# Expert outputs added into two sums by token in main memory, in place of four stored rows a token

## The chip, the cores and the metric

The kernel runs on one core of a Trainium2 chip. The metric is the device time of one execution in microseconds (us). Three timed runs of the kernel before gave 1543.5 us in the median (1541.84 to 1544.97).

## The reference, cut to what matters

The program is a network of four layers on 32 sequences of 128 tokens with 128 features (4096 tokens). Each layer is a gated cross-attention and a gated feed-forward part. The change is in the last feed-forward part, a mixture of 16 experts of which every token uses four:

```python
dist2 = jnp.sum((x[:, :, None, :] - keys) ** 2, axis=-1)
logits = -dist2 + jnp.einsum('bld,ed->ble', x, rw) + rb
topv, topi = jax.lax.top_k(logits, 4)
w = jax.nn.softmax(topv, axis=-1)
hidden = gelu(jnp.einsum('bld,efd->blef', x, w1) + b1)      # 16 experts, 512 wide
exp_out = jnp.einsum('blef,edf->bled', hidden, w2) + b2
fused = jnp.sum(w[..., None] * take_along_axis(exp_out, topi), axis=2)
x = x + tanh(g_ffn[3]) * fused
```

## The kernel before, in words

The stages are called A0, F0, A1, F1, A2, F2, A3, F3 (attention and feed-forward of layers 0 to 3). Each works on eight chunks c of four sequences (512 tokens), with the activations `x` held on chip. There is no scheduler: every engine has its own program, written out by hand, and they meet at semaphores. All loads and stores of plain blocks stand in SP's queue, in the order of its program. POOL issues the indirect DMAs.

**Routing** (`routing`, steps u = 6 to 14, on PE, ACT, DVE and POOL) runs beside A3, one chunk late. It picks four experts for each token, gives each of the four copies a place in a region of main memory that belongs to its expert (`dispatched_rows`), and POOL sends the rows there (`send`, L806, 16 indirect DMAs of 128 rows a chunk). A row is 128 features and one integer, the row of `expert_outputs` where its result belongs. The last chunk is done in two halves; the second one, called `routing(NC, ..., 1)`, runs inside F3. Steps 12 and 13 compute the places and release the send (`F3_rows_ready`), steps 12 and 14 the softmax weights, kept in `wt3`. The regions must be filled with an invalid row number first. SP does that with `prefill`: six regions of 2128.5 KB beside the stages before A2, and ten more right before the context loads of A2 (L532).

**F3** treats 144 tiles of 128 rows, each of one expert, in 12 groups of 12 slots. SP loads a tile (`load_tile`, L578). PE transposes it (`tile_T`, L1494), multiplies by the first weights (`up`, L1500) and by the second (`down`, L1508). DVE copies each tile's weights into place three tiles ahead (`weights`, L2752 to L2757) and adds the second bias when it takes the result (`output`, L2766). POOL scatters the result to `expert_outputs` (`scatter`, L843), one row for each token and expert, so no two scatters touch the same row. A slot is loaded again when its group of four scatters has landed.

**The end.** When all scatters have landed, SP loads the four rows of every token (L600, 8 loads of 1024 KB). For four chunks DVE does 16 multiply-adds each (L2806). For the four others, named in `MIXED3`, ACT builds 16 diagonal matrices of weights (`diagonals`, L1962), PE sums through them (L1548) and DVE adds the bank (L2800). SP stores each chunk of `x` (L605).

Of the kernel before, what the change touches and what calls it, by code (L numbers as in the profile page):

```python
# [5 lines left out]
F32 = mybir.dt.float32  # L6
# [8 lines left out]
B = 32  # L15
# [29 lines left out]
ROW3 = P + 1  # L45
# [23 lines left out]
MIXED3 = (1, 3, 5, 7)  # L69
# [72 lines left out]
def flamingo(nc, a, out):  # L142
    ctx = ExitStack()
    with ctx:
# [41 lines left out]
        mhalf = sb("mhalf", [P, CB])  # L186
        rstd = sb("rstd", [P, CB])
# [174 lines left out]
        wt3 = ar([P, B * TOP3])  # L362
# [18 lines left out]
        combined = arena[:, 0:NC * TOP3 * W].rearrange("p (c j k d) -> p c j k d", c=NC, k=TOP3, j=CB)  # L381
# [22 lines left out]

        def tile_bank(s):

            return bank[7 if s % 2 else 4]
# [13 lines left out]
        def diagonal(i, q):  # L421

            if i % 2 == 0:
                return flat_wqk3[:, q, :]
            return (flat_wv3 if q < SC // 2 else flat_wo3)[:, q % (SC // 2), :]

        sent = nc.dram_tensor("dispatched_rows", (UNUSED + P, ROW3), F32, kind="Internal").ap()
        sent_out = nc.dram_tensor("expert_outputs", (TOP3 * TOKENS, P), F32, kind="Internal").ap()
# [76 lines left out]
        def _(sp):  # L505
# [87 lines left out]
            for half in range(SLOTS3 // GROUP3):  # L593
                sp.wait_ge(sem(f"F3_scattered{half}"), GROUPS3 * GROUP3 * 16)
# [4 lines left out]
            for c in range(NC):  # L599
                sp.dma_start(combined[:, c, :, :, :].rearrange("t j k d -> t j (k d)"),  # L600
                             sent_out[c * W * TOP3:(c + 1) * W * TOP3, :].rearrange("(j t k) d -> t j (k d)", t=P, k=TOP3))\
                    .then_inc(sem(f"F3_outputs_loaded{c}"), 16)
# [7 lines left out]
        def _(pl):  # L610
# [13 lines left out]
            pl.memset(padf3[:, 0:P], 0.0)  # L624
            pl.memset(padu3[:, P:P + 1], int(NOWHERE)).then_inc(sem("F3_pad_row"), 1)
# [160 lines left out]
            pl.iota(goes3[:, :].rearrange("p (j k) -> p j k", j=CB), pattern=[[P * TOP3, CB], [1, TOP3]], base=0, channel_multiplier=TOP3,  # L786
# [44 lines left out]
            pl.wait_ge(sem("F3_prefilled"), 16 * (E3 + 1))  # L831
# [7 lines left out]
            def scatter(g, slots):  # L839
                for s in slots:  # L840
                    pl.wait_ge(sem("F3_output"), g * SLOTS3 + (s + 3))
                    pl.sem_inc(s_held, 1)
                    pl.indirect_dma_start(sent_out, bass.IndirectOffsetOnAxis(xtu3[:, s, P:P + 1], 0), yt3[:, s, :], None,  # L843
                                          bounds_check=TOP3 * TOKENS - 1, oob_is_err=False).then_inc(sem(f"F3_scattered{s // GROUP3}"), 16)
# [8 lines left out]
            send(range(SC // 2), 0)  # L853
            scatter(0, range(GROUP3))
# [10 lines left out]
        def _(pe):  # L865
# [675 lines left out]
            for i, c in enumerate(MIXED3):  # L1541
                pe.wait_ge(sem(f"F3_outputs_loaded{c}"), 16)
                pe.wait_ge(sem("F3_diagonals"), i + 1)
                if i >= 2:
                    pe.wait_ge(s_xdone, NC * STAGE["F3"] + 2 + MIXED3[i - 2])
                for j in range(CB):
                    for k in range(TOP3):
                        last = nc.tensor.matmul(bank[4 + i % 2][:, j * P:j * P + P], diagonal(i, j * TOP3 + k), combined[:, c, j, k, :],  # L1548
                                                start=(k == 0), stop=(k == TOP3 - 1))
                last.then_inc(sem("F3_mixed"), 1)  # L1550
# [3 lines left out]
        def _(act):  # L1554
# [399 lines left out]
            def diagonals(i):  # L1954

                if i >= 2:
                    act.wait_ge(sem("F3_mixed"), i - 1)
                if MIXED3[i] == NC - 1:
                    act.wait_ge(sem("F3_last_weights"), 1)
                for q in range(SC):  # L1960
                    at = MIXED3[i] * SC + q
                    last = nc.scalar.activation(diagonal(i, q), ident[:, :], ACT.Copy, scale=wt3[:, at:at + 1])  # L1962
                last.then_inc(sem("F3_diagonals"), 1)

# [28 lines left out]
            routing(NC, 10, 1)  # L1993
            for i in range(len(MIXED3)):
                diagonals(i)
# [3 lines left out]
        def _(dve):  # L1999
# [68 lines left out]
            def routing(c, u, half=None):  # L2068
                js = ALL if half is None else HALVES[half]
                n, of, qs = len(js), slice(js[0], js[-1] + 1), qs_of(js)  # L2070
                at, (_, tags, places) = route_bank(c, half), rows_of(half)
# [28 lines left out]
                if u == 10:  # L2100
# [5 lines left out]
                    if half is None:  # L2106
                        v.tensor_scalar(goes3[:, :], goes3[:, :], float(W * TOP3), None, ALU.add)
# [9 lines left out]
                if u in (12, 13):  # L2117
# [8 lines left out]
                    v.tensor_copy(places[:, qs], to3[:, qs]).then_inc(sem("F3_rows_ready"), 1)  # L2126
                if u in (12, 14):
# [4 lines left out]
                    kept = wt3[:, bass.ds(c * SC, SC)] if half is None else wt3[:, chunk * SC + qs.start:chunk * SC + qs.stop]  # L2132
                    last = v.tensor_tensor(kept.rearrange("p (j k) -> p j k", j=n), ex3[:, of, :],
                                           es3[:, of].unsqueeze(2).to_broadcast([P, n, TOP3]), ALU.mult)
                    if half == 1:
                        last.then_inc(sem("F3_last_weights"), 1)
                    else:
                        step(last)
# [127 lines left out]
            def heads3():  # L2266
# [47 lines left out]
                def last_body(c):  # L2314
                    for w in range(PAIRS):
# [3 lines left out]
                        if w in (3, 4, 5, 6, 7):  # L2319
                            routing(c - 1, {3: 7, 4: 8, 5: 9, 6: 10, 7: 13}[w])  # L2320
# [8 lines left out]
                def drain(c):  # L2329
                    routing(c - 2, 14)  # L2330
# [416 lines left out]
            def weights(n, s):  # L2747
# [7 lines left out]
                v.tensor_copy(b2c3[:, s % 4, :], b2b3[:, bass.ds(e * P, P)])  # L2755
# [4 lines left out]
            def output(n, s, g):  # L2760
# [3 lines left out]
                if g is not None:  # L2764
                    dve.wait_ge(sem(f"F3_scattered{s // GROUP3}"), g * (16 * GROUP3))
                v.tensor_tensor(yt3[:, s, :], bank[2 + s % 2][:, 0:P], b2c3[:, s % 4, :], ALU.add).then_inc(sem("F3_output"), 1)  # L2766
# [3 lines left out]
            for s in range(SLOTS3):  # L2770
# [5 lines left out]
                if s == 2:  # L2776
                    routing(NC, 13, 1)
# [7 lines left out]
            with dve.Fori(1, GROUPS3 - 1) as g:  # L2785
                for s in range(SLOTS3):
                    weights(g * SLOTS3 + (s + 3), s + 3)
# [7 lines left out]
            routing(NC, 14, 1)  # L2795

            for c in range(NC):
                if c in MIXED3:
                    dve.wait_ge(sem("F3_mixed"), MIXED3.index(c) + 1)
                    v.tensor_tensor(xc(c), xc(c), b4(4 + MIXED3.index(c) % 2), ALU.add).then_inc(s_xdone, 1)  # L2800
                    continue
                dve.wait_ge(sem(f"F3_outputs_loaded{c}"), 16)
                for k in range(TOP3):
                    for j in range(CB):
                        q = c * SC + j * TOP3 + k
                        last = v.scalar_tensor_tensor(xc(c)[:, j, :], combined[:, c, j, k, :], wt3[:, q:q + 1], xc(c)[:, j, :], ALU.mult, ALU.add)  # L2806
                    if k < TOP3 - 1:
# [31 lines left out]
```

## Time and profile before

| | before |
|---|---|
| median of 3 runs | 1543.5 us |
| the profiled execution | 1540.11 us |
| its span, first to last instruction | 1538.3 us |
| PE busy | 1364.3 us (89%) |
| DVE busy | 1107.5 us (72%) |
| POOL busy | 539.1 us (35%) |
| 144 scatters on POOL | 145.9 us busy, 120.6 us idle before them |
| DMA traffic | 98.30 MB |

The engines are PE (matrix products), DVE (vector), ACT (scalar functions), POOL and SP. Idle time of an engine that nobody waits for costs nothing, so the rows below are read by stage: which wait ends last there.

### The profile page before, as it was taken

How to read it: one execution, taken by the hardware profiler on the slowest of the kernel's cores; microseconds unless marked ns; L12 is line 12 of the kernel's file. 1: busy time of each engine (PE TensorE's matmuls, PEld its weight loads, DVE VectorE, ACT ScalarE, POOL GpSimd, SP SyncE). 2: the span in 40 equal slices, each digit the busy share in tenths (PEclk: the TensorE clock that was granted, in tenths of full speed). 3: DMA queues.
4: the chain of work that ended last, by engine and by line, in shares of the span. 5: the costliest groups of instructions: out<-in, count | busy, mean ns of one | idle time of the engine just before them, and what ended most of it. 6: DMA issues, size and time to landing. Idle time of an engine off the chain costs nothing.

```text
span 1538.3 us, 34321 instructions
## 1 busy us (share of the span) xinstructions
PE 1364.3 (89%) x9959; PEld 1021.1 (66%) x9982; DVE 1107.5 (72%) x3553; ACT 1001.9 (65%) x2922; POOL 539.1 (35%) x640
## 2 busy tenths in 40 slices
PE   4788887899989988999899999999997779999994
PEld 3566665677744456444566666666666679999994
DVE  4778888688777757886467777777778656666665
ACT  2688887554556556224777888888876446666665
POOL 3354359222211321001001522423423665555550
PEclk9999999999999999999999999999999899999998
DMA  8100039900199961000000100100032322222227
GB/s 200 26 8 7 8 56 161 140 0 1 49 169 161 165 102 35 1 0 0 8 9 1 36 24 13 36 23 14 29 142 112 89 72 66 64 67 67 64 59 274
DMA packets 143416, 98.30 MB, mean 64 GB/s; under 512 B 20597, under 2 KB 132514, under 8 KB 142154
## 3 DMA queue, kind: packets, MB, share of 16 engines
q1 hardware_dynamic: 134602, 80.09, 27.8%
q0 software_dynamic: 8704, 16.87, 3.3%
q8 instruction: 54, 0.88, 0.2%
q14 instruction: 56, 0.46, 0.1%
HBM read 43.03 MB, written 54.93 MB: 64 GB/s over the span
## 4 chain that ended last, share of the span: by engine, by line
PE 65%; ACT 12%; DVE 9%; issue 8%; POOL 3%; DMA 2%; SPq 1%; DVEq 0%; ACTq 0%; POOLq 0%
PE bank L1056 7%; PE bank L1500 7%; PE bank L1508 7%; PE bank L1072 4%; PE bank L1350 4%; ACT arena L1555 4%; PE bank L997 3%; ACT att L1692 3%; PE bank L1111 3%; PE bank L1060 3%; PE bank L1092 3%; ACT att L1557 2%; PE bank L1082 2%; PE bank L1426 2%; PE bank L979 2%
## 5 line engine op out<-in xcount | busy, mean ns | idle before, releaser
L1555 ACT ACTIVATE arena<-bank 128x512 f32<-128x512 f32 (+7 forms) x380 | 245.6, 675 | 150.2 <-PE bank L1413 54.1
L1972 ACT ACTIVATE att<-bank,arena 128x128 f32<-128x128 f32 x576 | 164.2, 368 | 89.9 <-PE bank L1500 89.9
L843 POOL DMA_INDIRECT expert_outputs<-arena x144 | 145.9, 1013 | 120.6 <-DVE arena L2766 102.8
L1692 ACT ACTIVATE att<-bank,arena 128x128 f32<-128x128 f32 x512 | 180.2, 394 | 11.6 <-DVE arena L2271 11.3
L806 POOL DMA_INDIRECT dispatched_rows<-arena x112 | 114.9, 1025 | 162.7 <-DVE arena L2126 114.0
L1500 PE MATMUL bank<-xnT,arena 128*128 128x128 f32 x1152 | 155.9, 279 | 3.7 <-DVE arena L2757 3.7
L639 POOL TENSOR_TENSOR ve<-mv,eps 128x4 f32<-128x4 f32 x64 | 12.8, 200 | 416.7 <-DVE mv L2042 407.3
L1508 PE MATMUL bank<-arena,att 128*128 128x128 f32 x1152 | 154.4, 278 | 0.3 <-ACT att L1972 0.3
L1500 PEld LDWEIGHTS bank<-xnT,arena 128*128 128x128 f32 x1152 | 143.4, 196 | 4.4 <-issue 3.1
L1508 PEld LDWEIGHTS bank<-arena,att 128*128 128x128 f32 x1152 | 142.4, 195 | 0.5 <-ACT att L1972 0.5
L1692 ACT ACTIVATION_READ_ACCUMULATOR att<-bank,arena 128x1 f32 x512 | 120.2, 235 | 0.0
L2752 DVE COPY arena<-arena 128x512 f32 x144 | 62.3, 433 | 78.7 <-issue 77.7
L1555 ACT ACTIVATE xnT<-bank 128x128 f32<-128x128 f32 (+1 forms) x180 | 63.6, 354 | 77.6 <-PE bank L881 41.5
L2271 DVE TENSOR_REDUCE arena<-bank 128x4 f32<-128x512 f32 x128 | 82.4, 685 | 43.9 <-PE bank L1072 43.9
L1677 ACT ACTIVATE arena<-bank 128x512 f32<-128x512 f32 x128 | 75.9, 613 | 55.5 <-PE bank L1056 55.5
L997 PE MATMUL bank<-ident,att 128*128 128x128 f32 x512 | 70.9, 283 | 32.5 <-ACT att L1557 32.0
L2156 DVE TENSOR_REDUCE nmx<-bank 128x8 f32<-128x1024 f32 x64 | 78.0, 1219 | 26.4 <-PE bank L968 25.9
L2277 DVE TENSOR_TENSOR att<-att,arena 128x512 f32<-128x512 f32 x128 | 89.2, 697 | 4.4
L997 PEld LDWEIGHTS bank<-ident,att 128*128 128x128 f32 x512 | 57.2, 144 | 49.4 <-ACT att L1557 48.7
L1350 PE MATMUL bank<-arena 128*128 128x512 f32 x192 | 87.6, 592 | 1.3 <-ACT arena L1555 0.9
L1072 PE MATMUL bank<-arena 64*128 64x128 f32 x1024 | 74.4, 284 | 12.9 <-ACT att L1692 6.5
L1072 PEld LDWEIGHTS bank<-arena 64*128 64x128 f32 x1024 | 62.3, 187 | 33.5 <-issue 24.8
(412 smaller groups left out, 3204.5 us busy)
## 6 DMA issues: line engine op xcount, KB each, us to landing
dispatched_rows<-padf SPq DMA_DIRECT2D x16, 2128.5 KB, 35.4
arena<-dispatched_rows SPq DMA_DIRECT2D x144, 64.5 KB
cxT<-in_ctx SPq DMA_DIRECT2D x32, 256.0 KB, 2.8
arena<-in_L_ffn_w SPq DMA_DIRECT2D x8, 1024.0 KB
arena<-expert_outputs SPq DMA_DIRECT2D x8, 1024.0 KB, 13.2
expert_outputs<-arena POOLq DMA_INDIRECT x144
out_x<-x SPq DMA_DIRECT2D x8, 256.0 KB, 4.2
dispatched_rows<-arena POOLq DMA_INDIRECT x112
```

The source lines that it names most:

```text
L806: pl.indirect_dma_start(sent, bass.IndirectOffsetOnAxis(places[:, q:q + 1], 0), held[:, q, :], None)\
L843: pl.indirect_dma_start(sent_out, bass.IndirectOffsetOnAxis(xtu3[:, s, P:P + 1], 0), yt3[:, s, :], None, bounds_check=TOP3 * TOKENS - 1, o ...
L997: last = nc.tensor.transpose(bank[2 + k][:, i * P:i * P + P], ex[:, v % 2 * 2 + k, i, :], ident[:, :])
L1056: last = nc.tensor.matmul(A[:, :], wqk3[:, t, pair * P:pair * P + P], cxT[:, p, :] if t else xnT[:, :], start=True, stop=True)
L1072: last = nc.tensor.matmul(bank[side][:, i * P:i * P + P], q, k, start=True, stop=True)
L1350: last = nc.tensor.matmul(bank[1 + j][:, :], xsT1[:, p * CB + j, t:t + P], wconv1[:, t, :], start=False, stop=(t == 2))
L1500: last = nc.tensor.matmul(bank[s % 2][:, k * P:k * P + P], w1c3[:, s % 4, k * P:k * P + P], xnT[:, (s % 4) * P:(s % 4) * P + P], start=Tru ...
L1508: last = nc.tensor.matmul(bank[2 + s % 2][:, 0:P], h3[:, s % 2, k * P:k * P + P], w2c3[:, s % 4, k * P:k * P + P], start=(k == 0), stop=(k ...
L1555: copy = lambda o, i: nc.scalar.activation(o, i, ACT.Copy)
L1692: last = nc.scalar.activation(ex3_of(w, side)[:, i, :], bank[side][:, i * P:i * P + P], ACT.Exp, bias=nm3[:, w % 2, h:h + 1], accum_out=su ...
L1972: last = nc.scalar.activation(h3[:, s % 2, k * P:k * P + P], bank[s % 2][:, k * P:k * P + P], ACT.Gelu, bias=b1c3[:, s % 4, k:k + 1])
L2277: v.tensor_tensor(ex3_of(w, side), ex3_of(w, side), rs3[:, w % 2, side:2 * HQ:2].unsqueeze(2).to_broadcast([P, HQ, P]), ALU.mult) .then_in ...
```

## The change

Results are weighted before they leave the chip, and the scatters add. A dispatched row has one more word, the weight, so routing computes the weights before it releases a send. DVE multiplies the result and the bias by the weight of each row. There are two sums of 4096 rows in main memory, filled with zeros by SP behind the ten regions. A scatter adds its rows into one of them, in turn by slot. Two additions into one sum may not overlap, so each scatter waits until the last but one has landed. At the end 16 loads of 256 KB bring in the two sums, and DVE adds them to `x`. The diagonals, PE's sums and the multiply-adds of the end are gone. The exponential of the last half chunk goes from ACT, after the tiles, to POOL, before its first scatter.

```diff
-ROW3 = P + 1
+ROW3 = P + 2
+SUMS3 = 2
+        def wait_scattered(eng, g, s):
+            last = s // SUMS3 + 1
+            if not isinstance(g, int):
+                eng.wait_ge(sem(f"F3_scattered{s % SUMS3}"), g * (16 * SLOTS3 // SUMS3) + 16 * last)
+            elif g * SLOTS3 // SUMS3 + last > 0:
+                eng.wait_ge(sem(f"F3_scattered{s % SUMS3}"), 16 * (g * SLOTS3 // SUMS3 + last))
...
                     prefill(range(PREFILLED_F0, E3))
+                    for view in sums_view:
+                        sp.dma_start(view, padf3[:, 0:P].unsqueeze(1).to_broadcast([P, B, P])).then_inc(sem("F3_prefilled"), 16)
...
                 for s in range(SLOTS3):
-                    if s % GROUP3 == 0 and not (isinstance(g, int) and g == 0):
-                        sp.wait_ge(sem(f"F3_scattered{s // GROUP3}"), g * (16 * GROUP3))
+                    if not (isinstance(g, int) and g == 0):
+                        wait_scattered(sp, g, s - SLOTS3)
                     load_tile(g * SLOTS3 + s, s)
...
             for c in range(NC):
-                sp.dma_start(combined[:, c, :, :, :].rearrange("t j k d -> t j (k d)"), ...
+                for k in range(SUMS3):
+                    sp.dma_start(summed3[:, c, k, :, :], sums_view[k][:, c * CB:(c + 1) * CB, :]).then_inc(sem(f"F3_outputs_loaded{c}"), 16)
...
                     pl.wait_ge(sem("F3_output"), g * SLOTS3 + (s + 3))
                     pl.sem_inc(s_held, 1)
-                    pl.indirect_dma_start(sent_out, bass.IndirectOffsetOnAxis(xtu3[:, s, P:P + 1], 0), yt3[:, s, :], None,
+                    wait_scattered(pl, g, s - SUMS3)
+                    pl.sem_inc(s_held, 1)
+                    pl.indirect_dma_start(sums_out[s % SUMS3], bass.IndirectOffsetOnAxis(xtu3[:, s, P:P + 1], 0), yt3[:, s, :], None,
+                                          bounds_check=TOKENS - 1, oob_is_err=False, compute_op=ALU.add)
...
             send(range(SC // 2), 0)
+            pl.wait_ge(sem("F3_less_max"), NC + 1)
+            pl.tensor_tensor(ex3[:, CB // 2:CB, :], base_e[:, :].rearrange("p (j k) -> p j k", k=TOP3), top3[:, CB // 2:CB, 0:TOP3], ALU.pow)
             scatter(0, range(GROUP3))
...
-                v.tensor_copy(b2c3[:, s % 4, :], b2b3[:, bass.ds(e * P, P)])
+                dve.wait_ge(sem(f"F3_tiles_loaded{slot // GROUP3}"), turn * (16 * GROUP3) + 16 * GROUP3)
+                v.tensor_scalar(b2c3[:, s % 4, :], b2b3[:, bass.ds(e * P, P)], xt3[:, slot, P + 1:P + 2], None, ALU.mult)
...
-                v.tensor_tensor(yt3[:, s, :], bank[2 + s % 2][:, 0:P], b2c3[:, s % 4, :], ALU.add)
+                v.scalar_tensor_tensor(yt3[:, s, :], bank[2 + s % 2][:, 0:P], xt3[:, s, P + 1:P + 2], b2c3[:, s % 4, :], ALU.mult, ALU.add)
...
             for c in range(NC):
+                for k in range(SUMS3):
+                    last = v.tensor_tensor(xc(c), xc(c), summed3[:, c, k, :, :], ALU.add)
```

On POOL, where F3 begins, before: the sends of the last chunk's first half, then four scatters (`expert_outputs`), four sends of the second half, and so on.

```order
L806 DMA dispatched_rows<-arena,last_places 67712x129 [waits F3_rows_copied,F3_rows_ready]
L806 DMA dispatched_rows<-arena,last_places 67712x129 x7
L843 DMA expert_outputs<-arena 16384x128 [waits F3_output] x4
L806 DMA dispatched_rows<-arena,last_places 67712x129 [waits F3_rows_copied,F3_rows_ready]
L806 DMA dispatched_rows<-arena,last_places 67712x129 x3
L843 DMA expert_outputs<-arena 16384x128 [waits F3_output] x4
```

The same place now:

```order
L811 DMA dispatched_rows<-arena,last_places 67712x130 [waits F3_rows_copied,F3_rows_ready]
L811 DMA dispatched_rows<-arena,last_places 67712x130 x7
L863 TENSOR_TENSOR arena<-base_e,arena 128x8 [waits F3_less_max]
L850 DMA expert_sums<-arena 4096x128 [waits F3_output] x2
L850 DMA expert_sums<-arena 4096x128 [waits F3_output,F3_scattered0]
L850 DMA expert_sums<-arena 4096x128 [waits F3_output,F3_scattered1]
L811 DMA dispatched_rows<-arena,last_places 67712x130 [waits F3_rows_copied,F3_rows_ready]
L811 DMA dispatched_rows<-arena,last_places 67712x130 x3
```

The power (L863) stands between the sends and the first scatter, and from the third scatter on each waits for an earlier one's landing.

On SP, before A2's loop of context loads (`cxT`), before:

```order
L523 DMA cxT<-in_ctx 128x4x128 [waits A12_v] x2
L532 DMA dispatched_rows<-padf 128x33x129 x10
L548 UNCONDITIONAL_BRANCH
L548 ISA
L523 ISA [waits A12_v]
L523 DMA cxT<-in_ctx 128x4x128
```

and now:

```order
L526 DMA cxT<-in_ctx 128x4x128 [waits A12_v] x2
L535 DMA dispatched_rows<-padf 128x33x130 x10
L552 DMA expert_sums<-padf 4096x1x128 x2
L553 UNCONDITIONAL_BRANCH
L553 ISA
L526 ISA [waits A12_v]
L526 DMA cxT<-in_ctx 128x4x128
```

Two fills of 2 MB stand ahead of the context load of A2's third chunk.

On DVE, the places of the last but one chunk (to `arena`, L2126), followed by the copy of an attention bank that PE waits for (L2285), before:

```order
L2124 TENSOR_TENSOR arena<-arena 128x256 [waits vector_steps]
L2125 TENSOR_REDUCE arena<-arena 128x16 [waits vector_steps]
L2126 CAST arena<-arena 128x16 [waits vector_steps]
L2285 COPY arena<-bank 128x512 [waits A3_pv]
L2276 RECIPROCAL arena<-arena 128x4 [waits A3_exp]
```

and now (the copy is L2266):

```order
L2111 TENSOR_TENSOR arena<-arena 128x256 [waits vector_steps]
L2112 TENSOR_REDUCE arena<-arena 128x16 [waits vector_steps]
L2113 CAST arena<-arena 128x16 [waits vector_steps]
L2115 TENSOR_REDUCE arena<-arena 128x4 [waits F3_exp,vector_steps]
L2116 RECIPROCAL arena<-arena 128x4 [waits vector_steps]
L2117 TENSOR_SCALAR arena<-arena,gates 128x4 [waits vector_steps]
L2118 TENSOR_TENSOR arena<-arena 128x16 [waits vector_steps]
L2266 COPY arena<-bank 128x512 [waits A3_pv]
L2257 RECIPROCAL arena<-arena 128x4 [waits A3_exp]
```

The four weight instructions, which stood behind the statistics of the next half, now stand between the places and PE's copy, and the send is released behind them.

## Rows read from the trace of the kernel before

**Rows 1.** Stretches: us, PE, PEld, DVE, ACT, POOL busy, clock, DMA share, GB/s

```profile
428.00:540.00 112.00, 101.93 (x456) 53.98 (x465) 82.04 (x316) 67.13 (x131) 25.74 (x44) 0.98 1.28 164
1300.00:1480.00 180.00, 180.00 (x1617) 179.98 (x1616) 120.00 (x476) 124.12 (x476) 96.50 (x95) 1.00 0.24 67
1510.00:1526.00 16.00, 10.21 (x71) 10.02 (x72) 11.54 (x39) 7.95 (x28) 0.00 (x0) 0.77 1.04 388
1528.00:1532.00 4.00, 2.51 (x23) 2.32 (x22) 3.93 (x14) 0.33 (x2) 0.00 (x0) 1.00 1.11 337
```

**Rows 2.** The chain that ended last, 1150 to 1540: start, us, what

```profile
1251.53 2.68 DMA expert_outputs<-arena
1258.69 1.98 DMA arena<-dispatched_rows
...
1502.35 2.13 DMA expert_outputs<-arena
1504.98 7.97 DMA arena<-expert_outputs
```

**Rows 3.** Timeline of two tiles: start, us, engine, line, operation, [idle before <-releaser]

```profile
1472.13 1.06 PE L1508 MATMUL bank<-arena,att 128*128 128x128 f32 x8
...
1474.03 1.06 PE L1508 MATMUL bank<-arena,att 128*128 128x128 f32 x8
```

**Rows 4.** Timeline of the end

```profile
1504.55 12.73 SPq L600 DMA_DIRECT2D arena<-expert_outputs  x8
1510.30 4.67 DVE L2806 SCALAR_TENSOR_TENSOR x<-arena,x 128x128 f32<-128x128 f32 x16 [7.97 <-DMA arena<-expert_outputs]
...
1534.40 0.69 DVE L2800 TENSOR_TENSOR x<-x,bank 128x512 f32<-128x512 f32 x1
```

**Rows 5.** Fills and context loads on SP, by line; PE's use of the third context

```profile
L532 SPq DMA_DIRECT2D dispatched_rows<-padf x16: 378/13332/15301, 221.6 to 528.6; - x16
...
DMA to landing us min/median/max: 2.6/2.8/10.1
...
552.32 4.09 SPq L523 DMA_DIRECT2D cxT<-in_ctx  x1
...
570.61 1.02 PE L1240 MATMUL bank<-cxT,wT 128*128 128x512 f32 x2
```

**Rows 6.** Timeline from A3 into F3, POOL

```profile
1187.26 1.44 POOL L806 DMA_INDIRECT dispatched_rows<-arena  x1 [19.38 <-DVE arena L2126]
...
1192.79 1.04 POOL L796 TENSOR_TENSOR rstd<-ve,mhalf 128x4 f32<-128x4 f32 x1
...
1227.11 1.00 POOL L843 DMA_INDIRECT expert_outputs<-arena  x1 [0.30 <-issue]
```

**Rows 7.** The same stretch, DVE and PE

```profile
1190.38 0.14 DVE L2129 TENSOR_REDUCE arena<-arena 128x4 f32<-128x16 f32 x1
...
1191.23 0.18 DVE L2133 TENSOR_TENSOR arena<-arena 128x16 f32<-128x16 f32 x1
...
1221.65 0.17 DVE L2126 CAST last_places<-arena 128x8 uint32<-128x8 f32 x1
1222.40 0.43 DVE L2752 COPY arena<-arena 128x512 f32 x1 [0.58 <-issue]
...
1239.61 0.33 PE L1494 MATMUL bank<-ident,arena 128*128 128x128 f32 x1 [3.91 <-DMA arena<-dispatched_rows]
...
1260.71 0.33 PE L1494 MATMUL bank<-ident,arena 128*128 128x128 f32 x1 [2.33 <-DMA arena<-dispatched_rows]
```

**Rows 8.** DVE by group, steady tiles, then F2: busy us, mean ns, idle before

```profile
L2766 DVE TENSOR_TENSOR arena<-bank,we 128x128 f32<-128x128 f32 x95 | 27.5, 290 | 5.2
L2755 DVE COPY we<-att 128x128 f32 x95 | 21.6, 227 | 0.0
...
L2662 DVE SCALAR_TENSOR_TENSOR x<-bank,arena,x 128x128 f32<-128x128 f32 x16 | 4.5, 343 | 3.0 <-PE bank L1434 3.0
L2623 DVE TENSOR_SCALAR xn<-x,mv,rstd 128x128 f32<-128x128 f32 x16 | 4.4, 343 | 0.2 <-POOL rstd L641 0.2
```

More of the change, by code:

```diff
@@ L186, in flamingo @@
         mhalf = sb("mhalf", [P, CB])
+        base_e = sb("base_e", [P, CB // 2 * TOP3])
         rstd = sb("rstd", [P, CB])
@@ L419, in qs_of @@
             return slice(js[0] * TOP3, (js[-1] + 1) * TOP3)
[L421 to L425, printed above, removed]
         sent = nc.dram_tensor("dispatched_rows", (UNUSED + P, ROW3), F32, kind="Internal").ap()
-        sent_out = nc.dram_tensor("expert_outputs", (TOP3 * TOKENS, P), F32, kind="Internal").ap()
+        sums_out = [nc.dram_tensor(f"expert_sums{k}", (TOKENS, P), F32, kind="Internal").ap() for k in range(SUMS3)]
+        sums_view = [s.rearrange("(p b) d -> p b d", p=P) for s in sums_out]
         rows = lambda ap, n=P: ap.rearrange("(a n) -> a n", a=1)[0].partition_broadcast(n)
@@ L592, in _ @@
                 load_group(g)
-            for half in range(SLOTS3 // GROUP3):
-                sp.wait_ge(sem(f"F3_scattered{half}"), GROUPS3 * GROUP3 * 16)
+            for k in range(SUMS3):
+                sp.wait_ge(sem(f"F3_scattered{k}"), 16 * (NT // SUMS3))
             s_out = sem("out_stored")
             for c in range(NC):
-                sp.dma_start(combined[:, c, :, :, :].rearrange("t j k d -> t j (k d)"),
-                             sent_out[c * W * TOP3:(c + 1) * W * TOP3, :].rearrange("(j t k) d -> t j (k d)", t=P, k=TOP3))\
-                    .then_inc(sem(f"F3_outputs_loaded{c}"), 16)
+                for k in range(SUMS3):
+                    sp.dma_start(summed3[:, c, k, :, :], sums_view[k][:, c * CB:(c + 1) * CB, :]).then_inc(sem(f"F3_outputs_loaded{c}"), 16)
             with sp.Fori(0, NC) as c:
@@ L624, in _ @@
             pl.memset(padf3[:, 0:P], 0.0)
+            pl.memset(padf3[:, P + 1:P + 2], 0.0)
+            pl.memset(base_e[:, :], 2.718281828459045)
             pl.memset(padu3[:, P:P + 1], int(NOWHERE)).then_inc(sem("F3_pad_row"), 1)
@@ L853, in _ @@
             send(range(SC // 2), 0)
+            pl.wait_ge(sem("F3_less_max"), NC + 1)
+            pl.tensor_tensor(ex3[:, CB // 2:CB, :], base_e[:, :].rearrange("p (j k) -> p j k", k=TOP3), top3[:, CB // 2:CB, 0:TOP3], ALU.pow)\
+                .then_inc(sem("F3_exp"), 1)
             scatter(0, range(GROUP3))
@@ L1540, in _ @@
                 down(n, s)
[L1541 to L1550, printed above, removed]
         @block.scalar
@@ L1952, in _ @@
             stage_start(act, STAGE["F3"])
[L1954 to L1963, printed above, removed]
             def tile_T(n, s):
@@ L1992, in _ @@
                     tile_T(n + 2, s + 2)
-            routing(NC, 10, 1)
-            for i in range(len(MIXED3)):
-                diagonals(i)
         @block.vector
@@ L2070, in routing @@
                 n, of, qs = len(js), slice(js[0], js[-1] + 1), qs_of(js)
-                at, (_, tags, places) = route_bank(c, half), rows_of(half)
+                at, (held, tags, places) = route_bank(c, half), rows_of(half)
                 chunk = c if half is None else NC - 1
@@ L2125, in routing @@
                     step(v.tensor_reduce(to3[:, qs], oh3[:, qs, :], AX, ALU.add))
-                    v.tensor_copy(places[:, qs], to3[:, qs]).then_inc(sem("F3_rows_ready"), 1)
-                if u in (12, 14):
+                    step(v.tensor_copy(places[:, qs], to3[:, qs]))
                     dve.wait_ge(sem("F3_exp"), c + 1)
@@ L2131, in routing @@
                     step(v.tensor_scalar(es3[:, of], es3[:, of], gates[:, 7:8], None, ALU.mult))
[L2132 to L2138, printed above, removed]
+                    v.tensor_tensor(held[:, qs, P + 1].rearrange("p (j k) -> p j k", j=n), ex3[:, of, :],
+                                    es3[:, of].unsqueeze(2).to_broadcast([P, n, TOP3]), ALU.mult).then_inc(sem("F3_rows_ready"), 1)
             def heads0():
@@ L2745, in _, with weights @@
             dve.sem_inc(sem("F3_output"), 2)
-            def weights(n, s):
+            def weights(n, s, g=None):
                 e = dve.value_load(tab3[0:1, 0, bass.ds(n, 1)], min_val=0, max_val=E3 - 1)
@@ L2754, in weights @@
                     dve.wait_ge(sem("F3_output"), n - 1)
-                v.tensor_copy(b2c3[:, s % 4, :], b2b3[:, bass.ds(e * P, P)])
+                slot = s % SLOTS3
+                turn = (n // SLOTS3 if isinstance(n, int) else g + s // SLOTS3)
+                dve.wait_ge(sem(f"F3_tiles_loaded{slot // GROUP3}"), turn * (16 * GROUP3) + 16 * GROUP3)
+                v.tensor_scalar(b2c3[:, s % 4, :], b2b3[:, bass.ds(e * P, P)], xt3[:, slot, P + 1:P + 2], None, ALU.mult)
                 v.tensor_copy(b1c3[:, s % 4, :], b13[:, :, :].rearrange("p e k -> p (e k)")[:, bass.ds(e * K3, K3)])
@@ L2764, in output @@
                 if g is not None:
-                    dve.wait_ge(sem(f"F3_scattered{s // GROUP3}"), g * (16 * GROUP3))
-                v.tensor_tensor(yt3[:, s, :], bank[2 + s % 2][:, 0:P], b2c3[:, s % 4, :], ALU.add).then_inc(sem("F3_output"), 1)
+                    wait_scattered(dve, g, s - SLOTS3)
+                v.scalar_tensor_tensor(yt3[:, s, :], bank[2 + s % 2][:, 0:P], xt3[:, s, P + 1:P + 2], b2c3[:, s % 4, :], ALU.mult, ALU.add)\
+                    .then_inc(sem("F3_output"), 1)
             for n in range(3):
@@ L2776, in _ @@
                 if s == 2:
-                    routing(NC, 13, 1)
+                    routing(NC, 12, 1)
                 if s == 4:
@@ L2786, in _ @@
                 for s in range(SLOTS3):
-                    weights(g * SLOTS3 + (s + 3), s + 3)
+                    weights(g * SLOTS3 + (s + 3), s + 3, g)
                     output(g * SLOTS3 + s, s, g)
@@ L2793, in _ @@
                 output(n, s, GROUPS3 - 1)
-            routing(NC, 14, 1)
             for c in range(NC):
[L2798 to L2807, printed above, removed]
+                dve.wait_ge(sem(f"F3_outputs_loaded{c}"), 16 * SUMS3)
+                for k in range(SUMS3):
+                    last = v.tensor_tensor(xc(c), xc(c), summed3[:, c, k, :, :], ALU.add)
+                    if k < SUMS3 - 1:
                         step(last)
```

17 lines of the change are left out of this document (7 added, 10 removed).

## The prediction

> **What bounds the kernel now.** I read four views. First the table of stretches [rows 1]. Between 1300 and 1480 us PE is busy all the time, so the steady tiles are bound by PE; two products of neighbouring tiles start 1.90 us apart [rows 3]. POOL works half of that time and no other engine sets the pace. The same table shows the end as a stretch of DMA: from 1510 to 1526 us the queues move 388 GB/s at a full share, while PE and DVE idle. Then the chain of waits [rows 2]: it runs through two landings of scatters, one at 1251.53 us in the restart of F3 and the last one at 1502.35 us, followed by 7.97 us of waiting for the first load. Then the timelines of the two places where the chain leaves PE: the end [rows 4], and the way from A3 into F3, where POOL's queue is late [rows 6, 7]. Last the DMA queue of SP in front of A2 [rows 5]. So the change acts in four places: the end, the 144 scatters, the restart of F3, and A2's loads. The profiled execution took 1540.11 us, 3.4 us below the median of 1543.5; the sum is made against the first and its difference is carried to the median.
>
> **The end: what goes.** Now the last scatter starts at 1502.35, lands 2.13 later, SP issues at 1504.55, DVE gets the first chunk at 1510.30 (5.75 later) and finishes the last one at 1535.09; the span ends 3.2 us behind that, at 1538.3 [rows 2, 4]. Afterwards 16 loads carry 4.19 MB in place of 8.39. I take 3.2 us for the landing of an adding scatter (below), so SP issues at 1505.6. The first chunk is 0.52 MB instead of 1.05; at 388 GB/s [rows 1] the missing 0.52 MB are 1.4 us, so DVE starts 4.4 us behind, at 1510.0. A chunk costs DVE two additions of 128x512 at 0.69 us [rows 4], with a short wait between them 1.45 us; eight are 11.6, until 1521.6. The loads don't hold it up: 4.19 MB at 388 GB/s are 10.8 us from about 1506.6. With the 3.2 us for the last store the span ends at 1524.8. Gain: 13.5 us. If the landing stays at 2.1 it is 14.6. A floor to it: all bytes, 4.19 MB at 388 and 2.10 MB of stores at 337 GB/s, take 17 us, so the end can't come before 1523.
>
> The stores of the end, 256 KB each, ran at 337 GB/s one behind another [rows 1]. The Trainium skill, "DMA: Bandwidth & Descriptors", section "Rules for kernel authors", asks for at least 1 MiB a DMA; by that rule the 16 small loads would be the wrong exchange for 8 of 1 MB. The trace speaks against it here, since small stores overlap, and it stands among the rivals.
>
> **The 144 scatters: a new wait.** A scatter now starts only when the last but one has landed, so two are under way at most. What is queued behind the waiting one on POOL is the next scatter; SP's load of the slot and, 12 tiles later, DVE's output wait for its landing. With landing time L and the gap of 0.30 us between two indirect DMAs on POOL [rows 6], a pair takes L + 0.3, a tile half of it. PE wants a tile each 1.90, so the wait is hidden up to L = 3.5. A plain scatter lands in 2.13 to 2.68 us [rows 2]. No row shows one that adds. It must also read its rows from main memory. Lower bound: nothing more than the plain one, 2.1. Upper bound: a whole load in series with it; the quickest one of a context took 2.6 from issue to landing [rows 5], so 2.7 + 2.6 = 5.3. The reads come inside one DMA and share its start and its receipt, so I take a value nearer to the plain row: 3.2, hidden with 0.3 to spare. Both ends stay for the range: each us of L above 3.5 costs half a us on each of 144 tiles, 72 us.
>
> For the read alone the Trainium skill, same page, section "Latency and other measured facts", gives a main memory latency of 0.2 us on average and 2 us at high load; by it L would be an estimated 2.3 to 4.7, on both sides of the limit. No run here shows it.
>
> DVE's part of a tile grows: the bias copy of 227 ns becomes a multiplication by a column (343 in the nearest row), the output goes from 290 to 343 [rows 8]. That is 0.17 us a tile. DVE is busy 120.0 of 180 us [rows 1], 1.27 of 1.90 a tile, and copies weights three tiles ahead, so I take nothing; if DVE's waits in between can't shrink, it costs up to 0.1 on each tile, 14 us. The new wait for a tile's load in front of the bias asks for it one tile earlier than PE does; in the steady tiles the load is long there.
>
> **From A3 into F3.** POOL's sends of the last but one chunk start when its places are ready (19.38 us of waiting on DVE L2126 before 1187.26 [rows 6]). Now the four weight instructions come first: from 1190.38 to 1191.41 us, 1.03 us [rows 7]. DVE, PE and POOL are late by that until F3; the same four are gone later, but there DVE waits for POOL. Cost 1.0. The same step in the earlier chunks only gains a wait on DVE of about 0.1 us each: 0.5 in all.
>
> Then POOL's power. It sits behind eight sends that end at 1226.8 us, in front of the first scatter at 1227.11 [rows 6]. A power over 4 columns takes 1.04, over 8 columns between that and 2.08; I take 1.6. DVE arrives at the place that now waits for it at 1221.8 [rows 7], so DVE stands still for some 8 us, and behind it weights and outputs of tiles 3 and on. PE runs dry for as long. But PE stands there before too: 3.91 us at 1239.61 and 2.33 at 1260.71 for loads that wait for POOL's scatters [rows 7], and the chain of waits goes through POOL, so what counts is when the twelfth scatter lands. POOL's queue to it gains 1.0 (above), 1.6 (power), and three waits for landings (scatters 3, 7 and 11): each start comes L + 0.3 = 3.5 after the one two before, in place of 2 x 1.29 = 2.58 by POOL's own pace, 0.9 each, 2.7. The landing itself gains 0.5 on 2.68. Against that SP now waits scatter by scatter: before, from that landing (1254.2) to PE's start (1260.71) four loads were issued, 6.5 us; now only the last one is left, about 1.3 of issue and 1.98 of landing [rows 2], 3.3. Sum: 1.0 + 1.6 + 2.7 + 0.5 - 3.2 = 2.6 us. With L = 2.1 it is about -1, with L = 3.5 about 4.
>
> **A2's loads.** Two fills of 2.10 MB go into SP's queue ahead of the load of A2's third context. Before, SP issued that load at 552.32, held up 4.09 us by the fills ahead, and it landed 10.1 us behind its issue, the longest of its kind [rows 5], at 562.4; PE needs it at 570.61. So 8.2 us are free. The old fills write rows of 516 bytes at 164 GB/s, the stores of whole 512-byte rows ran at 337 [rows 1]. Two fills cost 12.4 us at the second rate, 25.6 at the first. The new rows are whole 512 bytes, so I take the second: PE waits 12.4 - 8.2 = 4.2 us, and A2 is bound by PE there. Ends: 0 and 17.
>
> **The sum.** -13.5 + 4.2 + 2.6 + 0.5 = -6.2 us. From 1540.11 to 1533.9 for a profiled execution, from 1543.5 to 1537.3 in the median: 1537. Without the uncertain wait its own range is 1528 (no stall in A2, L = 2.1) to 1545.
>
> **The rivals.**
> - *The pair of scatters becomes the bound.* Place: POOL's wait for the last but one landing. For it: an addition must read what it changes, and the margin is only 0.3 us of an unknown. Against it: the landing that the trace shows leaves 0.8 to 1.4 us for the read. It decides from L = 3.5 on. At L = 4.2 the 144 tiles take 0.35 us longer each, +50: about 1585. At the upper bound of 5.3 it is +130: about 1665. PE would show idle time in every second tile, and scatters would start evenly L + 0.3 apart by pairs.
> - *The fills are as slow as the old ones.* Place: SP's queue before A2. For it: it is the same broadcast of the same tile, same queue. Against it: whole rows. PE waits 17 us in place of 4.2: 1550, slower by 0.4%.
> - *Sixteen small loads don't overlap.* A context load of the same 256 KB takes 2.6 us alone [rows 5]; 16 in a row are 41.6, so the span would end near 1552, 14 us later than before: 1564. Against it: the stores at 337 GB/s. [...]
> - *The end gains and the front costs nothing:* 1528 to 1530, if SP's fills pass unnoticed and POOL's waits are free.
>
> **How the numbers follow.** Forecast, wait hidden: 0.50 (with the costless front, which is its lower edge). Pair of scatters as the bound: 0.34, most of it between 1545 and 1600, 0.13 above. Slow fills: 0.11. Small loads: 0.05. A measurement of this kernel can tell 0.2%, 3 us, from no change: faster is below 1540.4, slower above 1546.6. Of the forecast's 0.50 some 0.07 fall within; L just above 3.5 adds to both sides. Faster 0.47, same 0.12, slower 0.41. The range takes in the forecast, the slow fills and the scatters up to L = 4.4: 1527 to 1600; about 0.03 lie below and 0.14 above.
>
> **What would show it.** In the profile after: steady tiles at 1.90 us with PE busy throughout (hidden), or PE waiting on DVE, DVE on landings (bound). POOL's idle time before a scatter, put down to DVE or to a landing. In A2 a wait of PE for a context near 571 us, of 4 us. DVE waiting for POOL's power for 8 us, and PE's third wait for tile loads ending near 1267. From the last landing to the end of the span 19 us, in place of 33.8. I am wrong if L is above 3.5, or if the two fills take more than 20 us.

## The result and the profile after

The changed kernel takes 1568.6 us (median of 4 runs, 1567.5 to 1570.0), the kernel before beside it 1542.7 (4 runs, 1539.2 to 1545.0): ratio 1.0174, 95% interval 1.0158 to 1.0190. It is slower by 1.7%; the forecast was 1537, faster. The profiled execution has a span of 1566.9 us, 28.6 more than before's 1538.3. The table of stretches, with the columns of [rows 1]:

```profile
428.00:540.00 112.00, 101.89 (x451) 53.68 (x460) 82.29 (x316) 67.52 (x131) 26.61 (x46) 0.98 1.25 184
1300.00:1480.00 180.00, 170.03 (x1464) 165.23 (x1462) 119.07 (x428) 115.28 (x432) 136.44 (x86) 1.00 0.47 60
1546.00:1562.00 16.00, 0.00 (x0) 0.00 (x0) 10.59 (x16) 0.00 (x0) 0.00 (x0) 0.50 0.98 320
```

The second row is the result in one line. PE was busy for all 180 us of this stretch in [rows 1]; now it is idle for 10 of them and gets through 1464 matmuls in place of 1617. POOL issues 86 scatters in place of 95, one each 2.09 us against 1.89, and is busy for 136 us instead of 96.5. The clock is 1.00 in both, so this isn't the clock.

The end did gain. Its timeline (start, us, engine, line, operation, [idle before <-releaser]); L850 is the scatter (L843 before), L605 SP's loads of the sums, L2782 DVE's additions:

```profile
1533.63 1.55 POOL L850 DMA_INDIRECT expert_sums<-arena  x1 [0.91 <-DMA expert_sums<-arena]
1535.03 0.35 DVE L2749 SCALAR_TENSOR_TENSOR arena<-bank,arena,we 128x128 f32<-128x128 f32 x1 [1.14 <-PE bank L1519]
...
1542.90 1.55 POOL L850 DMA_INDIRECT expert_sums<-arena  x1 [0.30 <-issue]
1545.68 8.41 SPq L605 DMA_DIRECT2D arena<-expert_sums  x16
1549.29 1.42 DVE L2782 TENSOR_TENSOR x<-x,arena 128x512 f32<-128x512 f32 x2 [13.91 <-DMA arena<-expert_sums]
1552.55 9.47 DVE L2782 TENSOR_TENSOR x<-x,arena 128x512 f32<-128x512 f32 x14 [1.84 <-DMA arena<-expert_sums]
```

From the start of the last scatter to the end of the span it is 24.0 us, before 36.0 [rows 2]: 12.0 gained. But the last scatter starts 40.6 us later than the 1502.35 of [rows 2], and 7.5 us after DVE's last output (1535.38), where before it followed within 0.9: POOL ends with a queue of its own. 40.6 - 12.0 is the 28.6 of the span. Of the 40.6, the first scatter (1229.46 against 1227.11 [rows 6]) brings 2.4; the 143 intervals behind it bring 38.2. The first 24 of these, the restart of F3, take 62.4 us in place of 50.6 and bring 11.8; the other 119 bring 26.4, 0.22 each.

How POOL waits, in its timeline of the steady tiles:

```profile
1396.76 1.55 POOL L850 DMA_INDIRECT expert_sums<-arena  x1 [0.62 <-issue]
1398.74 1.56 POOL L850 DMA_INDIRECT expert_sums<-arena  x1 [0.43 <-issue]
1400.89 1.55 POOL L850 DMA_INDIRECT expert_sums<-arena  x1 [0.59 <-issue]
1402.80 1.55 POOL L850 DMA_INDIRECT expert_sums<-arena  x1 [0.36 <-issue]
1405.07 1.61 POOL L850 DMA_INDIRECT expert_sums<-arena  x1 [0.73 <-issue]
```

Two things stand here. An adding scatter takes POOL 1.55 us; the plain one took 0.98 to 1.00 [rows 6]. And scatters two apart start 4.06 to 4.18 us apart. The releaser named is "issue", not a landing, and one could conclude that POOL waits for nothing. The release came, but while POOL still worked on the scatter in between, so it leaves no idle time of its own; what is left is the way from the release to the start. A chain of waits shows landings of such scatters, and what they hold up:

```profile
1381.02 3.53 DMA expert_sums<-arena
1384.66 0.27 SPq L582
1384.96 0.15 SPq L582
1385.36 2.38 DMA arena<-dispatched_rows
...
1542.90 2.72 DMA expert_sums<-arena
```

From POOL's start to the landing it is 3.53 us here, where [rows 2] had 2.68 and 2.13; most other landings on that chain took 3.3 to 3.7, and the extremes are the 2.72 of the last one and one of 4.18. SP waits for it to reload the slot, and the load is late for PE and DVE. From the waits of 1240 to 1536 us (engine, line, what it waited for: us in total, times, longest):

```profile
DVE we L2738 <- DMA arena<-dispatched_rows: 40.0, 32, 5.0
PEld bank L1505 <- DMA arena<-dispatched_rows: 29.5, 32, 4.6
...
PE bank L1505 <- DMA arena<-dispatched_rows: 23.1, 29, 4.4
```

L1505 is PE's transposition of a tile (L1494 before, which had the waits of 3.91 and 2.33 us of [rows 7] and none in the steady tiles). So the picture is the first rival: scatters bound the stage. Which part of a scatter does it, the trace alone doesn't settle.

### The profile page after: what moved, and what is told of

Same layout as the page of the kernel before. It is cut to its first block, busy times and chain, and to the rows that moved or that the text cites. A ratio compares the mean times of both kernels' runs of the same rounds, so it can differ in the third digit from the quotient of the medians.

```text
span 1566.9 us, 34347 instructions
## 1 busy us (share of the span) xinstructions
PE 1361.8 (87%) x9831; PEld 1010.9 (65%) x9854; DVE 1114.1 (71%) x3501; ACT 984.9 (63%) x2856; POOL 626.4 (40%) x643
## 4 chain that ended last, share of the span: by engine, by line
PE 49%; issue 12%; ACT 12%; DVE 10%; POOL 9%; DMA 5%; DVEq 1%; SPq 1%; POOLq 1%; ACTq 0%
PE bank L1067 7%; POOL expert_sums L850 7%; PE bank L1083 4%; PE bank L1361 4%; ACT arena L1556 4%; PE bank L1008 3%; DMA expert_sums<-arena 3%; PE bank L1122 3%; ACT att L1693 3%; PE bank L1071 3%; PE bank L1103 3%; ACT att L1558 2%; PE bank L1093 2%; PE bank L990 2%; PE bank L1437 2%
## 5 line engine op out<-in xcount | busy, mean ns | idle before, releaser
L850 POOL DMA_INDIRECT expert_sums<-arena x144 | 228.0, 1583 | 76.9 <-issue 51.5
L1693 ACT ACTIVATE att<-bank,arena 128x128 f32<-128x128 f32 x512 | 180.2, 394 | 11.6 <-DVE arena L2252 11.2
L811 POOL DMA_INDIRECT dispatched_rows<-arena x112 | 118.2, 1055 | 160.2 <-DVE arena L2118 120.4
L1511 PE MATMUL bank<-xnT,arena 128*128 128x128 f32 x1152 | 159.0, 282 | 10.9 <-DVE arena L2740 10.9
L1511 PEld LDWEIGHTS bank<-xnT,arena 128*128 128x128 f32 x1152 | 144.1, 196 | 12.5 <-issue 11.5
L2732 DVE COPY arena<-arena 128x512 f32 x144 | 68.1, 473 | 63.0 <-issue 61.8
L1083 PE MATMUL bank<-arena 64*128 64x128 f32 x1024 | 74.4, 284 | 12.1 <-ACTq L1685 6.3
```

The source lines that it names most:

```text
L811: pl.indirect_dma_start(sent, bass.IndirectOffsetOnAxis(places[:, q:q + 1], 0), held[:, q, :], None)\
L850: pl.indirect_dma_start(sums_out[s % SUMS3], bass.IndirectOffsetOnAxis(xtu3[:, s, P:P + 1], 0), yt3[:, s, :], None, bounds_check=TOKENS - ...
L1083: last = nc.tensor.matmul(bank[side][:, i * P:i * P + P], q, k, start=True, stop=True)
L1511: last = nc.tensor.matmul(bank[s % 2][:, k * P:k * P + P], w1c3[:, s % 4, k * P:k * P + P], xnT[:, (s % 4) * P:(s % 4) * P + P], start=Tru ...
L1693: last = nc.scalar.activation(ex3_of(w, side)[:, i, :], bank[side][:, i * P:i * P + P], ACT.Exp, bias=nm3[:, w % 2, h:h + 1], accum_out=su ...
```

## The experiments

Theory A: the chain of waits. A scatter starts 0.83 us behind the landing of the one two before and lands 3.3 us after its start; two in flight make (0.83 + 3.3) / 2 = 2.07 us a tile against PE's 1.90. Rival B: POOL's own 1.55 us and the 0.47 of sequencer work that the chain shows between two scatters, 2.02 us whatever is in flight. Rival C: DVE, with its weighted bias and its new wait for the tile's load. Rival D, for the restart: DVE's wait for POOL's power makes PE late to the end.

### Four sums

```diff
-SUMS3 = 2
+SUMS3 = 4
```

> Four sums in place of two; all else as in the changed kernel, so its loads at the end are 8.4 MB again and its fills 8.4 MB. Theory A (each scatter waits for the landing of the one two before it: 0.10 us to the release, 0.73 us to the start of the adding scatter on POOL, 3.3 us to its landing, so (0.83 + 3.3) / 2 = 2.07 us a tile against 1.90 of TensorE): with four sums the chain allows 1.04 us a tile, the tiles come back to 1.90 us, POOL has no backlog at the end, and of the 1568.6 us go 24.6 (120 tiles of 0.205) and 6.7 (backlog), while 4.2 MB more at 286 GB/s add 14.7 to the end: 1552. Rival B (POOL itself: 1.55 us of an adding scatter and 0.47 of its sequencer make 2.02 us a tile whatever the number of sums): the tiles stay above 2.0 us, about 1574. Rival C (VectorE's new wait for the tile load and its weighted bias): the pace stays 2.095, about 1583.

1546.2 us (4 runs), ratio to before 1.0042 (1.0027 to 1.0058). The steady stretch, and two scatters in it:

```profile
1300.00:1480.00 180.00, 180.00 (x1617) 180.00 (x1616) 130.61 (x475) 124.21 (x475) 151.04 (x96) 1.00 0.51 67
```

```profile
1397.44 1.55 POOL L850 DMA_INDIRECT expert_sums<-arena  x1 [0.30 <-issue]
1399.30 1.55 POOL L850 DMA_INDIRECT expert_sums<-arena  x1 [0.31 <-issue]
```

PE is busy for 180 of 180 us again, and POOL runs a scatter of the same 1.55 us after 0.30 us, 1.85 a tile. That refutes B: the 0.47 was part of the way from a release, not of POOL's pace. It refutes C: all of DVE's new work and its new wait are still there (130.6 us busy against 120.0 [rows 1]), and PE doesn't notice. Theory A stands. It missed by about 6 us: the end grew by 10.8 us (34.8 from the last scatter to the end of the span in place of 24.0) and not by 14.7, and the last scatter starts 34.0 us earlier, where 31.3 was taken. The landing is no quicker with four in flight:

```profile
DMA to landing us min/median/max: 2.7/3.3/3.9
```

### Three sums

```diff
-SUMS3 = 2
+SUMS3 = 3
```

> Three sums. Theory A: the chain allows (0.83 + 3.3) / 3 = 1.38 us a tile, below 1.90, so the tiles are back at 1.90 us as with four sums; the end loads 6.3 MB, 7.3 us more than with two: 1568.6 - 24.6 - 6.7 + 7.3 = 1545. Rival B (POOL's own 2.02 us a tile): about 1567. Rival C (VectorE's wait for the load): about 1576.

1542.7 us (10 runs), ratio 1.0011 (1.0001 to 1.0020). PE is busy for 180 of 180 us here too; from the last scatter to the end it is 30.2 us, between the 24.0 of two sums and the 34.8 of four. A's 1545 is the nearest.

### Two tensors, no addition

```diff
-                                          bounds_check=TOKENS - 1, oob_is_err=False, compute_op=ALU.add).then_inc(sem(f"F3_scattered{s % SUMS3}"), 16)
+                                          bounds_check=TOKENS - 1, oob_is_err=False).then_inc(sem(f"F3_scattered{s % SUMS3}"), 16)
```

> Two tensors and all waits as in the changed kernel, but the scatters write and don't add: what it leaves out is the adding (each token keeps the row written last). Theory A: an unadding scatter landed in 2.1 to 2.7 us before the change, so the chain allows (0.83 + 2.4) / 2 = 1.6 us a tile and TensorE's 1.90 holds: 1568.6 - 24.6 - 6.7 = 1537. If the landing into the two small tensors stays at 3.3 us, theory A says no change (1568), and rival B (POOL's 1.55 us, which falls to 0.99) still says 1537. Rival C (VectorE's wait for the load): 1568 either way.

1527.0 us (4 runs), ratio 0.9921 (0.9904 to 0.9937). Its steady stretch:

```profile
1300.00:1480.00 180.00, 180.00 (x1617) 180.00 (x1616) 127.80 (x476) 124.39 (x476) 98.12 (x95) 1.00 0.25 67
```

The same tensors, fills, rows with weights, loads and waits, without the addition: 41.6 us less than the changed kernel by the medians, 39 by the two ratios. On the chain of waits its scatters land in 2.13 to 2.49 us (one in 3.16), as in this row:

```profile
1398.49 2.17 DMA expert_sums<-arena
```

So the small tensors don't lengthen the landing; it is the addition that makes the wait bind. The expectation was 10 us too high, since it gave back the steady tiles and the queue at the end only. The restart comes back too: its last scatter starts at 1500.4, 2 us ahead of before.

### One sum

```diff
-SUMS3 = 2
+SUMS3 = 1
```

> One sum: every scatter waits for the landing of the one just before it. Theory A, with the price of a link taken from the two-sum trace (0.83 us from landing to POOL's start, 3.3 us to the landing): 143 x 4.14 = 592 us from the first scatter at 1229 to the last, some 8 us less where the last tiles are empty (2.7 us to land), and 16.7 us from the last scatter to the end: about 1845. If a landing is quicker with nothing else in flight (2.7 us): 143 x 3.5 = 505, about 1755. Rival B (POOL's own 2.02 us a tile): about 1560.

1850.1 us (one run); A's sum was 1845, B's 1560. With one scatter in flight the chain of waits shows each link by itself (POOLq is POOL's sequencer):

```profile
1502.05 0.03 POOLq L850
1502.08 0.47 issue
1502.55 0.03 POOLq L846
...
1502.71 0.03 POOLq L409
1502.74 0.03 issue
1502.78 3.38 DMA expert_sums<-arena
1506.15 0.02 issue
1506.18 0.02 POOLq L849
...
1506.98 3.13 DMA expert_sums<-arena
```

POOL starts at 1502.78, the scatter has landed at 1506.16, POOL starts the next at 1506.98: 3.38 and 0.82 us. Of the second, 0.1 passes before the sequencer comes to the scatter (L850); the other 0.7 are the sequencer's steps and the pauses named "issue" between them, the longest 0.47. Two such links overlapped are the 2.09 us of the changed kernel.

### The power earlier

```diff
-            send(range(SC // 2), 0)
+            send(range(1), 0)
             pl.wait_ge(sem("F3_less_max"), NC + 1)
...
+            send(range(1, SC // 2), 0)
```

> The changed kernel with POOL's power for the last half-chunk's weights put behind the first of the eight sends in place of behind the eighth. VectorE's wait of 6.05 us for it should go to under 1 us. Theory A (the chain of scatters sets the end, and it starts when POOL is free): only what POOL itself saves counts, 1.7 to 2.5 us, 1566 to 1567. Rival D (the late restart of TensorE is handed down whole to the end): 7 us, 1561.5.

1566.4 us (5 runs), ratio 1.0174 (1.0159 to 1.0188) to a before of 1540.9. That is 2.3 less than the changed kernel's 1568.6, but the ratio of that one, to a before of 1542.7, is 1.0174 too: these times don't tell a gain of 2 us from none. D's 1561.5 would be a ratio of 1.0134, outside the interval. In the changed kernel DVE waited for the power, and the first scatter stood behind it:

```profile
1227.60 1.67 POOL L863 TENSOR_TENSOR arena<-base_e,arena 128x8 f32<-128x8 f32 x1
1229.37 0.16 DVE L2115 TENSOR_REDUCE arena<-arena 128x2 f32<-128x8 f32 x1 [6.05 <-POOL arena L863]
1229.46 1.64 POOL L850 DMA_INDIRECT expert_sums<-arena  x1 [0.20 <-issue]
```

Now it runs where POOL stood idle, between the first send and the second, and DVE has no wait for it:

```profile
1217.37 1.67 POOL L863 TENSOR_TENSOR arena<-base_e,arena 128x8 f32<-128x8 f32 x1 [0.89 <-DVE arena L2099]
1219.64 1.04 POOL L811 DMA_INDIRECT dispatched_rows<-arena,last_places  x1 [0.60 <-issue]
```

From the start of the first of the eight sends to the first scatter it was 14.5 us (1214.94 to 1229.46) and is now 13.1 (1215.51 to 1228.59), so POOL's queue is 1.4 us shorter. 6.05 us of DVE's waiting went, and the time doesn't show them. D falls; that POOL's queue counts, as A has it, agrees with the runs, but its 1.7 to 2.5 us are too few for these times to show.

### Three sums and the early power

The two edits above together.

> Three sums and POOL's power behind the first of the eight sends. With three sums TensorE is 5.5 us late from tile 24 to the end, against its own start of the stage. If POOL's queue makes that (sixteen sends, the first scatters at 1.55 us in place of 0.99 and the power), the earlier power takes 1.7 to 2.2 us off: 1540.5. If VectorE's wait of 7.3 us for the power makes it, all 5.5 us go: 1537.

1541.6 us (12 runs), ratio 1.0009 (0.9999 to 1.0019). A gain of 5.5 us over three sums alone is excluded (1537 would be a ratio of 0.998); the 1.1 us measured don't tell POOL's 2 from nothing. It is no slower and no faster than before.

### A sum that retires early

For the last twelve tiles the scatters go to the second and third sum alone; SP loads the first one behind the last tile load, and DVE adds it while it waits for the others.

```diff
+                    k = s % SUMS3 if not (isinstance(g, int) and g == LAST) else 1 + s % 2
...
+            sp.wait_ge(sem("F3_scattered0"), 16 * BEFORE3)
+            for c in range(NC):
+                sp.dma_start(first_sum(c), sums_view[0][:, c * CB:(c + 1) * CB, :]).then_inc(sem("F3_first_sum"), 16)
```

> Three sums in turn up to tile 131, then the last twelve tiles go to the second and third alone, and the first is loaded behind the last tile load, while TensorE works, and added before the other two arrive. Early power too. The chain for twelve tiles in two sums is 2.07 us a tile at 3.3 us to land and (0.83 + 2.72) / 2 = 1.78 where the tiles are empty, as the last ones are, so no time is lost there; the end is that of two sums, 24.0 us from the last scatter in place of 30.2. Against three sums with the early power: 6 us less, 1534.5, 4 to 6 us faster than the kernel before. If the preload of 2.1 MB disturbs the tile loads or the last links are 2.07 us, 2 to 4 us of it are lost.

1541.7 us (11 runs), ratio 1.0009 (1.0000 to 1.0019): nothing gained. The end is indeed short, 24.6 us, but POOL comes to it late. Its timeline, with SP's eight loads issued from 1497.66 to 1501.41:

```profile
1494.32 1.80 POOL L864 DMA_INDIRECT expert_sums<-arena  x1 [0.70 <-DVE arena L2766]
1497.12 1.55 POOL L864 DMA_INDIRECT expert_sums<-arena  x1 [1.00 <-DMA expert_sums<-arena]
1498.98 1.55 POOL L864 DMA_INDIRECT expert_sums<-arena  x1 [0.30 <-issue]
1503.33 1.55 POOL L864 DMA_INDIRECT expert_sums<-arena  x1 [2.80 <-DMA expert_sums<-arena]
```

POOL waits 2.80 us for a landing as the loads go out, and at 1.85 us a scatter it can't make up for it: its last scatter starts 9.1 us behind DVE's last output, 3.5 in the version above. The profiled execution took 1547.8 us, 6.1 above the median of the eleven, so its waits are on the long side.

### The same with its loads spread

```diff
             for c in range(NC):
+                sp.wait_ge(sem(f"F3_scattered{1 + c % 2}"), 16 * (BEFORE3 + c // 2 + 1))
                 sp.dma_start(first_sum(c), sums_view[0][:, c * CB:(c + 1) * CB, :]).then_inc(sem("F3_first_sum"), 16)
```

> As the retired sum, but its eight loads of 256 KB are no longer issued in one burst behind the last tile load: load c waits for the landing of scatter 132 + c. In the burst three scatters in a row waited 1.0, 2.8 and 1.7 us for landings, POOL ended 9.1 us behind VectorE (3.5 with three sums), and the 6 us of the shorter end were gone. If the burst's contention made that, the lag falls back to about 3 us and the time to 1536, 0.3% faster than the kernel before. If the two sums' chain in the last twelve tiles made it, the lag stays at 7 to 9 us and the time at 1541.

1542.4 us (12 runs), ratio 1.0011 (0.9999 to 1.0024), POOL's lag 8.4 us: my theory of the burst falls. Now four separate scatters wait 0.8 to 1.8 us for landings. With two sums there is no slack in the chain for anything else on the queues, burst or not. How much of the lag the two sums make by themselves can be estimated from the changed kernel, which has no such loads there: its last twelve intervals between scatters took 25.2 us, against 22.4 with three sums and the early power, 27.9 with the spread loads and 29.3 with the burst. By this some half of what the spread version lost on its last twelve tiles is the chain of two sums alone.

No version that adds beat the kernel before: three sums with the early power is level with it.

## Why the prediction was wrong, by its own steps

**The 144 scatters: the step that failed.** The mechanism was told rightly, and its price L too: I took 3.2 us, the traces show a median of 3.3 (2.7 to 3.9 with four sums). What failed is "the gap of 0.30 us between two indirect DMAs on POOL". [Rows 6] has that gap for a scatter whose wait is long over. For one that is released by its wait the gap is 0.83. That it was readable before the change is the sharper lesson; the timeline of the kernel before:

```profile
1401.19 0.29 DVE L2766 TENSOR_TENSOR arena<-bank,we 128x128 f32<-128x128 f32 x1
1402.33 1.10 POOL L843 DMA_INDIRECT expert_outputs<-arena  x1 [0.91 <-DVE arena L2766]
```

DVE's output ends at 1401.48, and the scatter that it releases starts 0.85 us later, tile after tile. With 0.85 the limit is L = 2 x 1.90 - 0.85 = 2.95 in place of 3.5, and my own L lies 0.25 above it: at 72 us per us of L, +18. With the measured 3.3 and 0.83 it is +24; behind the restart the scatters took 26.4 us more. A forecast with a chance of 0.50 hung on a margin of 0.3 us, and the gap alone was wrong by 0.55.

A second term was missing: POOL's own time for an adding scatter, 1.55 us against 0.98. I had put the whole price of the addition into the landing. In the steady tiles it hides (1.55 + 0.30 is below 1.90), but in the restart POOL's queue is the path, and each of the first scatters is 0.56 us longer.

The Trainium skill ("DMA: Bandwidth & Descriptors", "Latency and other measured facts") gives a main memory latency of 0.2 us on average and 2 us at high load. The landing fits between the two: a median of 3.3 us against 2.13 to 2.68 [rows 2] is 0.6 to 1.2 more. No run shows the read by itself.

**The end: right.** 12.0 us against 13.5. DVE's additions came as forecast (10.9 us busy for 11.6), but the span ends 4.9 us behind them, where 3.2 was taken. The sixteen loads of 256 KB, with the first stores, moved 320 GB/s from 1546 to 1562 us, and with four sums the loads alone moved 394:

```profile
1520.00:1528.00 8.00, 0.00 (x0) 0.00 (x0) 7.72 (x12) 0.00 (x0) 0.00 (x0) 0.50 1.05 394
```

That is as much as the 388 of [rows 1], where the loads were of 1 MB, so the rival of small loads fell. By the size rule of the Trainium skill ("DMA: Bandwidth & Descriptors", "Rules for kernel authors"), at least 1 MiB a DMA for the most bandwidth, they should have moved less; with many in flight these rows show no such loss. The prediction also calls PE and DVE idle in that stretch of [rows 1]; its row has them busy for 10.2 and 11.5 of the 16 us.

**From A3 into F3.** The power took 1.67 us for 1.6, and its shift took 1.4 out of POOL's queue. DVE waited 6.05 us for it where 8 was said. The prediction was right that such a wait on DVE counts little. The sum of 2.6 was still too low: the first 24 intervals between scatters alone bring 11.8 us. Two things are in it: the first scatters' 0.56 us each, and links of 4.1 us a pair for 3.5. Four sums tell them apart; here is the 25th scatter of the changed kernel and of that one:

```profile
1291.87 1.55 POOL L850 DMA_INDIRECT expert_sums<-arena  x1 [0.34 <-issue]
1283.76 1.57 POOL L850 DMA_INDIRECT expert_sums<-arena  x1 [0.30 <-issue]
```

Behind the first scatter (at 1229.46 and 1228.41) that is 62.4 and 55.4 us, where the kernel before took 50.6. With four sums the scatters follow each other at 0.30 us and no landing holds them up, so of the 11.8 us the links of two sums make 7.1, and 4.8 stay with the longer scatters.

**DVE's part of a tile: right at nothing.** Four sums show it.

**A2's loads: 4.2 us forecast, nothing came.** SP's queue before A2:

```profile
516.44 12.68 SPq L535 DMA_DIRECT2D dispatched_rows<-padf  x1
529.16 20.40 SPq L552 DMA_DIRECT2D expert_sums<-padf  x2
551.28 43.72 SPq L526 DMA_DIRECT2D cxT<-in_ctx  x7
```

The last of the old fills is issued at 516.4, before at 528.6 [rows 5]. Its rows are 520 bytes long in place of 516, and its median in the queue fell from 13.3 us [rows 5] to 12.1; the stretch moved 184 GB/s in place of 164. The old fills gave back what the new ones cost, and the context is issued at 551.28, earlier than the 552.32 of [rows 5]. What the prediction didn't see is that SP, its fills issued, waited 9.0 us in front of that load before, until PE let go of the buffer; now it waits 1.4. I had priced the new fills by their row length and left the changed length of the old rows out. Four fills moved that issue to 559.1. The slowest context load there landed 9.6 us behind its issue, so this one was there by 568.7, at most 6.3 us later than before, and PE still had no wait for a context: the 8.2 us free agree with it.

**The chances.** The first rival had 0.34 and was read as the nearest danger; 1568.6 lies inside the range, and in the part that the rival's chance put between 1545 and 1600.

## What to carry to other kernels

A wait on the last but one landing is a chain, and its link is the landing plus the way from a release to the start of the next instruction. Read both from rows in which an instruction was released by a wait, never from instructions that follow each other without one. Where a price fits under a limit by less than the error of its parts, add a second buffer of slack to the change or call it even: a third sum took some 25 us off.

## What was not expected of the hardware

- An indirect DMA that adds costs POOL 1.55 us for 128 rows of 512 bytes, 0.98 without the addition, and lands a median of 3.3 us after its start with one, three or four in flight at most (2.7 to 3.9 with four; one of 4.18 on the changed kernel's chain), against 2.13 to 2.68 [rows 2].
- From the end of a wait to the start of an indirect DMA on POOL: 0.82 to 0.86 us in three kernels; 0.30 between two where nothing is waited for.
- The profile names "issue" as the releaser where a wait ended while the engine was still at work on its last instruction, though the wait sets the pace.
- A broadcast fill of 2.1 MB spent 1.3 us less in the queue with rows of 520 bytes than with 516 (12.1 against 13.3 median). Why wasn't tried.
